# A two-layer vision tower on one core: divided softmax chain, one-pass products, moved turnings, zero products and an early weight split

## Chip, cores, metric

One core of a Trainium2 chip. The metric is the device time of one execution in microseconds, as the median of several runs.

## What is computed

Eight images of 256 x 256 are cut into 64 patches of 1024 values; a linear layer makes 192 features of each and a class token goes in front, so there are 8 x 65 = 520 tokens. Two layers follow, each with attention and an expert layer, each behind a layer norm and added to the stream `h`:

```
h = h + L0_attn(norm(h))   # squared scores plus scores, no softmax
h = h + L0_ffn(norm(h))    # 8 experts of width 768, top 2, gelu
h = h + L1_attn(norm(h))   # 12 heads of 16, all tensors quantized to 8 bits
h = h + L1_ffn(norm(h))    # 8 experts of 128 and 8 of 256, top 8, gelu
```

The second attention quantizes queries, keys, values and scores by global minimum and maximum, and its softmax is an integer one:

```
x_int = round(x / scale); x_int = x_int - max(x_int, axis=-1)
x0_int = floor(-LN2 / scale); x_int = maximum(x_int, N_EXP * x0_int)
qexp = floor(x_int / x0_int); r = x_int - x0_int * qexp
b_int = floor(b / a / scale); c_int = floor(c / a / (scale * scale))
e = (r * (r + b_int) + c_int) * exp2(-qexp) * (a * scale * scale)
return e / sum(e)
```

## The kernel before

The program is written out by hand, one instruction stream for each engine, with semaphores between them; the order of the text is the order on the engine. There is no planner. In a VectorE stream `then` issues a step and waits for its end, `settle` issues and only counts, `step` issues and gives the count, and `after` waits for such a count.

**Expert layers.** `ffn` goes through 48 tiles of 128 hidden columns in the first layer and 24 in the second. A tile has two halves of 260 tokens. TensorE makes the hidden values (`entry`), ScalarE the gelu, VectorE multiplies with the token's weight (L1301), ScalarE and VectorE split the product in a high and a low fp32r part (L998, L1306), and TensorE multiplies down (`project`, L597 and L659). Products in fp32r are one pass of TensorE, and the pair of parts replaces an fp32 product. TensorE's order is the up product of tile x + 2, then the down product of tile x. The weights come by DMA into one of two raw slots, one load for each first-layer expert, and are split the same way by `weights_hi` on ScalarE (L974, L976) and `weights_lo` on VectorE (L1282, L1285), three pieces for a load: the pieces of load n + 1 stand in the first three tiles of load n. Load 0 is split during the first attention. SyncE issues the loads, each behind the semaphore that its slot's last low part has raised; the first layer's load 3 stands behind the combine weights (`comb_to_dram`, `token_weights`).

**Softmax.** The scores lie in `sc`: 50 rows of 65 for each partition, two rows for the class token's queries and 48 for the patches' (12 for each of four pairs of images). For them there are four chunks, 14 rows and three times 12. While the scores come in nine groups, VectorE reduces maximum and minimum (L1507, L1508). TensorE turns the two statistics, VectorE reduces them and TensorE spreads the result (`statistics`). Then a chain of steps on one or three elements gives the scale, its reciprocal, the factor `alpha`, bounds, and the integer constants (L1512 to L1540). For each chunk ScalarE scales (L1122; GpSimd chunk 3), VectorE subtracts the row's top and clamps (`distance`, L1553 and L1554), ScalarE makes the quotient (L1128), GpSimd the power of two (L541; ScalarE chunk 3), VectorE the remainder (L1561), ScalarE the square (L1134), and VectorE the exponential (L1573). Its end raises `e_ready`: the first time behind the class rows' normalisation (L1597 to L1599), which are divided at once; the others are divided after the product.

**Products with the values.** TensorE turns a chunk's pair rows with fp32 transposes (`turn_rows`: L835 the class rows, L846 six blocks of 128, L849 the left-over first and last keys of an image, 6 rows for each parity), ScalarE and VectorE copy them out of PSUM, and `times_v` multiplies: L858 left-over keys with `v_last` (408 columns, fp32), L861 six blocks with `v_pairs`. `times_v_cls` (L871) has 16 fp32 products of 12 columns for the class token. An fp32 product stands as two records in the profile. `output` on VectorE divides and reduces for the next statistics (L1611 to L1619); L1634 to L1637 do so for the class token. `v_pairs` and `v_last` are made earlier, by ScalarE and GpSimd (L531, L533).

**Zero products.** `fill(n)` issues n bf16 products of a zero matrix with 260 zero columns, whose result nobody reads. They stand ahead of several transposes of normalised rows. Ahead of the second routing there are 50. The routing (`gate`, `route`) multiplies by the router in fp32 and turns the logits (L590).

## Time and profile before

| | us |
|---|---|
| median of 3 runs | 371.45 (371.27 to 372.63) |
| the profiled execution | 371.17 |
| its span, first to last instruction | 369.1 |
| TensorE products, busy | 298.1 (81%) |
| VectorE, busy | 268.8 (73%) |
| ScalarE, busy | 202.3 (55%) |
| GpSimd, busy | 20.8 (6%) |
| mean granted TensorE clock | 0.882 |

The profiled execution takes 2.1 us more than its span; that part lies before the first and after the last instruction. A busy share is a mean over stages with different limits: what a stage is bound by is read from its own stretch. Times in the rows are counted from the span's start. Each row of a timeline is start, duration, engine, line, operation and operands; in square brackets stands the idle time of the engine before it and who ended that.

### The profile page before, as it was taken

The page shows a single profiled execution, that of the slowest core. Times are in us where ns is not written, and L with a number is a line of the kernel's source. Part 1 is how long each engine was busy: PE and PEld are TensorE (multiplying, and loading weights), DVE is VectorE, ACT ScalarE, POOL GpSimd, SP SyncE. Part 2 cuts the span into 40 slices and gives each one's busy share as a digit, 9 for nine tenths or more (in the row PEclk, how much of TensorE's full clock was granted, in tenths as well). Part 3 has the DMA queues.
Part 4 walks back from the last instruction along what each step waited for, and adds up shares of the span by engine and source line. Part 5 has one row for each costly group of instructions (what it writes and reads, how often), then busy time and mean ns, then how long its engine had stood idle before and what let it go on. Part 6 is the DMA issues. An engine that isn't in the chain of part 4 may idle for free.

```text
span 369.1 us, 6068 instructions
## 1 busy us (share of the span) xinstructions
PE 298.1 (81%) x2294; PEld 267.2 (72%) x2294; DVE 268.8 (73%) x717; ACT 202.3 (55%) x486; POOL 20.8 (6%) x46
## 2 busy tenths in 40 slices
PE   5989998899999999999881260099439888999991
PEld 5968857799999999999781140067326278999991
DVE  1269275888888888898668989965468558888852
ACT  1034476677677686777273574660010667777750
POOL 4230000000000000000000015400000000000000
PEclk9999999999999999999996555578557699999997
DMA  6980401235044043000000000000500014444401
GB/s 201 302 275 3 151 0 45 92 133 178 16 166 168 13 151 99 2 1 2 2 0 0 2 2 0 0 2 0 199 0 3 0 33 125 149 154 134 114 7 43
DMA packets 10396, 27.37 MB, mean 74 GB/s; under 512 B 1368, under 2 KB 1992, under 8 KB 10368
## 3 DMA queue, kind: packets, MB, share of 16 engines
q1 hardware_dynamic: 9792, 26.03, 21.9%
q0 software_dynamic: 576, 0.96, 1.2%
q8 instruction: 18, 0.29, 0.3%
q14 instruction: 10, 0.08, 0.1%
HBM read 26.54 MB, written 0.45 MB: 73 GB/s over the span
## 4 chain that ended last, share of the span: by engine, by line
PE 65%; DVE 25%; ACT 5%; issue 2%; DMA 1%; DVEq 0%; ACTq 0%
PE bank L597 26%; PE bank L659 9%; PE bank L577 7%; PE bank L644 4%; PE bank L642 4%; PE bank L700 3%; PE bank L861 2%; PE bank L846 1%; DVE embed_area L1553 1%; ACT hid_hi L998 1%; DVE bn L1204 1%; PE bank L858 1%; DVE group_lo L1508 1%; DVE row_hi L1507 1%; DVE stat_q L1428 1%
## 5 line engine op out<-in xcount | busy, mean ns | idle before, releaser
L597 PE MATMUL bank<-hid_hi,pj_parts 128*128 128x260 f32 x288 | 76.1, 285 | 1.7 <-DVE hid_lo L1306 1.7
L998 ACT ACTIVATE hid_hi<-hidden_area 128x260 fp32r<-128x260 f32 x144 | 55.9, 422 | 38.8 <-DVE hidden_area L1301 37.5
L1306 DVE TENSOR_TENSOR hid_lo<-hidden_area,hid_hi 128x260 fp32r<-128x260 f32 x144 | 56.6, 427 | 10.0 <-ACT hid_hi L998 0.9
L597 PEld LDWEIGHTS bank<-hid_hi,pj_parts 128*128 128x128 f32 x288 | 54.1, 188 | 2.5 <-DVE hid_lo L1306 2.0
L991 ACT ACTIVATE hidden_area<-bank 128x260 f32<-128x260 f32 x144 | 49.2, 377 | 5.7 <-PE bank L644 4.7
L597 PE MATMUL bank<-xt_hi,fc_hi 128*128 128x260 f32 x144 | 41.6, 289 | 1.4 <-ACT hidden_area L989 1.3
L644 PE MATMUL bank<-xt_lo,fc_lo 128*128 128x260 f32 x144 | 41.4, 288 | 0.0
L659 PE MATMUL bank<-hid_hi,pj_parts 128*128 128x260 f32 x144 | 40.7, 283 | 0.0
L659 PE MATMUL bank<-hid_lo,pj_parts 128*128 128x260 f32 x144 | 40.7, 282 | 0.0
L597 PE MATMUL bank<-hid_lo,pj_parts 128*128 128x260 f32 x144 | 40.7, 282 | 0.0
L597 PE MATMUL bank<-xt_lo,fc_hi 128*128 128x260 f32 x144 | 40.7, 282 | 0.0
L642 PE MATMUL bank<-xt_lo,fc_hi 128*128 128x260 f32 x144 | 40.6, 282 | 0.0
L597 PE MATMUL bank<-xt_hi,fc_lo 128*128 128x260 f32 x144 | 40.4, 281 | 0.0
L1301 DVE TENSOR_TENSOR hidden_area<-hidden_area 128x260 f32<-128x260 f32 x72 | 28.0, 424 | 7.0 <-ACT hidden_area L989 6.1
L1301 DVE TENSOR_TENSOR hidden_area<-hidden_area,xn 128x260 f32<-128x260 f32 x72 | 28.1, 423 | 2.2 <-ACT hidden_area L991 1.7
L597 PEld LDWEIGHTS bank<-xt_hi,fc_hi 128*128 128x128 f32 x144 | 27.2, 189 | 1.9 <-ACT hidden_area L989 1.5
L1282 DVE TENSOR_TENSOR fc_lo<-raw_area,fc_hi 128x768 fp32r<-128x768 f32 (+1 forms) x28 | 23.5, 844 | 5.4 <-ACT fc_hi L974 4.3
L597 PEld LDWEIGHTS bank<-hid_lo,pj_parts 128*128 128x128 f32 x144 | 27.3, 190 | 0.0
L597 PEld LDWEIGHTS bank<-xt_lo,fc_hi 128*128 128x128 f32 x144 | 27.1, 189 | 0.1
L597 PEld LDWEIGHTS bank<-xt_hi,fc_lo 128*128 128x128 f32 x144 | 27.1, 188 | 0.0
L659 PEld LDWEIGHTS bank<-hid_lo,pj_parts 128*128 128x128 f32 x144 | 27.1, 188 | 0.0
L659 PEld LDWEIGHTS bank<-hid_hi,pj_parts 128*128 128x128 f32 x144 | 27.1, 188 | 0.0
(299 smaller groups left out, 571.0 us busy)
## 6 DMA issues: line engine op xcount, KB each, us to landing
raw_area<-fc_dram SPq DMA_DIRECT2D x8, 768.0 KB, 4.3
raw_area<-pj_dram SPq DMA_DIRECT2D x8, 576.0 KB, 5.4
xn<-comb_dram SPq DMA_DIRECT2D x12, 260.0 KB, 3.4
raw_area<-fc_dram SPq DMA_DIRECT2D x6, 512.0 KB, 4.1
embed_area<-embed_in_dram SPq DMA_DIRECT2D x8, 352.0 KB, 8.2
hidden_area<-comb_dram SPq DMA_DIRECT2D x9, 260.0 KB, 3.3
raw_area<-pj_dram SPq DMA_DIRECT2D x6, 384.0 KB, 4.4
score_area<-w_l_dram SPq DMA_DIRECT2D x1, 576.0 KB, 11.8
```

The source lines that it names most:

```text
L577: last = pe.matmul(out, lhs(kc), rhs(kc), start=(kc == 0), stop=(kc == KC - 1))
L597: mm = pe.matmul(out, lhs[a], rhs[b], start=start and n == 0, stop=stop and n == 2, skip_group_check=True)
L642: pe.matmul(out, fc_hi[:, s, 1, cols], x_mix[:, tok], start=False, stop=False, skip_group_check=True)
L644: mm = pe.matmul(out, fc_lo[:, s, 1, cols], x_mix[:, tok], start=False, stop=True, skip_group_check=True)
L659: mm = pe.matmul(PB[SUMS[2 + n]][:, 0:HALF], pj_tails[:, s, j], hidden[:, x % 3, tok], start=x == 0 and part == 0, stop=part == 1, skip_gr ...
L700: mm = pe.matmul(PB[i][:, 0:D], patches[:, k, i * 128:(i + 1) * 128], w_tok[:, k, :], start=(k == 0), stop=(k == TOKK - 1))
L861: last = pe.matmul(PB[4 + i][:, k * 4 * (HD + 1):(k + 1) * 4 * (HD + 1)], e_t[:, HC * i + k, :], v_pairs[:, i, 2 * k:2 * k + 2, :, :].rear ...
L991: act.activation(hid[:, x % 2, tok], src, ACT.Gelu_apprx_tanh).then_inc(entry_out[y], 1)
L998: act.activation(hid_hi[:, x % 3, tok], hid_w[:, x % 2, tok], ACT.Copy).then_inc(hid_hi_ready[y], 1)
L1282: dve.tensor_tensor(lo, raw, hi.bitcast(F32), ALU.subtract).then_inc(w_lo_done[s], 1)
L1301: dve.tensor_tensor(hid_w[:, x % 2, tok], hid[:, x % 2, tok], tok_w[tile.weights][:, tok], ALU.mult).then_inc(weighted[y], 1)
L1306: dve.tensor_tensor(hid_lo[:, x % 3, tok], hid_w[:, x % 2, tok], hid_hi[:, x % 3, tok].bitcast(F32), ALU.subtract).then_inc(hid_lo_ready[y ...
```

## The change

1. *Early split.* All six pieces of load 1 are split during the first attention: the high parts behind those of load 0 on ScalarE, the low parts on VectorE between the squared scores and the residual update. Tiles 0 to 2 of the first expert layer have no pieces left.
2. *Scalar chain.* `qk` and `qk_step` are made among the nine groups of reductions. The bound below (`sa_lo`) is gone: scores and tops are only cut from above. The integer constants run interleaved with the tops, and their last five steps (`exp_floors`) stand between the two halves of chunk 0's distance.
3. *Order of the chunks.* VectorE makes chunk 0's exponential and the class rows ahead of chunk 1's remainder and chunk 3's distance. ScalarE copies the class rows and chunk 0's turned rows between the squares and quotients.
4. *One-pass products.* Exponentials of the class rows and the left-over keys are split into a high part (ScalarE's copy) and a low part (VectorE: `e_cls_lo`, `e_last_lo`), both fp32r. The low part of the left-over keys takes 38 further partitions, at 64 and up, against the same values, so L858 is one fp32r product; `v_last` then has 102 partitions, and the turning of these values four small products instead of two. The low part of the class rows takes 12 further columns, so the 16 class products have 24 columns each, in fp32r, and the mask has 24.
5. *Order on TensorE.* In `times_v` the left-over keys come last. `times_v(0)` stands before the third turning, `times_v(1)` before the fourth.
6. *Zero products.* 36 ahead of the first turning, from the first quotient on, and 5 ahead of the second. Ahead of the second routing 46, then a wait for the variances, then 14, instead of 50.
7. *Places.* Some tensors lie elsewhere (`v1_flat` in `hid_hi`, `e_cls` and `e_last` in `hid_lo`, `logits_t` in the hidden area).

```diff
-LR = 38
+LR = 102
+TWICE = 2 * 12
...
+        v1_flat = hid_hi[0:S].rearrange("p a c -> p (a c)")[:, 0:B * D].rearrange("p (b d) -> p b d", b=B)
...
+        hid_lo_words = hid_lo[:].rearrange("p a c -> p (a c)")
+        e_cls = hid_lo_words[0:S, 0:256].rearrange("p (r q) -> p r q", r=2)
+        e_last = hid_lo_words[0:LR, 256:768].rearrange("p (i q) -> p i q", i=4)
...
+        v_last = sb("v_last", [LR, 4, NH, 2, HD + 1], F32R)
...
-        o_cls_m = sb("o_cls_m", [DC, B * KC, NH])
+        o_cls_m = sb("o_cls_m", [DC, B * KC, TWICE])
...
-                                    pe.matmul(bank[0:m, at:at + DC // 2], even, own[0], start=True, stop=True)
-                                    last = pe.matmul(bank[m:z, at:at + DC // 2], odd, own[1], start=True, stop=True)
+                                    at = ((b % 4) * KC + kc) * (DC // 2)
+                                    for row, n_rows, key, q in ((0, 32, 0, 0), (32, 32, S - 1, 1), (64, 32, 0, 0), (96, HC, S - 1, 1)):
+                                        last = pe.matmul(bank[row:row + n_rows, at:at + DC // 2],
+                                                         v[:, key:key + 1].broadcast_to([DC, n_rows]), own[q],
+                                                         start=True, stop=True)
...
-                    pe.wait_ge(e_cls_ready, 1)
+                    pe.wait_ge(e_cls_lo_ready, 1)
                 if c >= 2:
                     pe.wait_ge(et_act, ET_ACT[c - 2])
+                    pe.wait_ge(e_last_lo_ready, 2 * (c - 1))
...
+                for k in range(HC):
+                    pe.matmul(PB[4 + i][:, k * 4 * (HD + 1):(k + 1) * 4 * (HD + 1)], e_t[:, HC * i + k, :],
+                              v_pairs[:, i, 2 * k:2 * k + 2, :, :].rearrange("p h b d -> p (h b d)"),
+                              start=k == 0, stop=False, skip_group_check=True)
                 pe.wait_ge(v_last_ready, 5 * (i + 1))
+                pe.wait_ge(e_last_lo_ready, 2 * (i + 1))
                 pe.matmul(PB[4 + i][:, 0:PAIR_COLS], e_last[:, i, :], v_last[:, i].rearrange("p h b d -> p (h b d)"),
-                          start=True, stop=False, skip_group_check=True)
-                for k in range(HC):
-                    last = pe.matmul(PB[4 + i][:, k * 4 * (HD + 1):(k + 1) * 4 * (HD + 1)], e_t[:, HC * i + k, :],
-                                     v_pairs[:, i, 2 * k:2 * k + 2, :, :].rearrange("p h b d -> p (h b d)"),
-                                     start=False, stop=True, skip_group_check=True)
-                last.then_inc(pv_mm, 1)
+                          start=False, stop=True, skip_group_check=True).then_inc(pv_mm, 1)
...
-                        at = (2 * b + kc) * NH
-                        last = pe.matmul(PB[1][0:DC, at:at + NH], v1_flat[:, b, kc * DC:(kc + 1) * DC],
-                                         e_cls[:, b // 4, SLOT * (b % 4):SLOT * (b % 4) + NH], start=True, stop=True)
+                        at = (2 * b + kc) * TWICE
+                        last = pe.matmul(PB[1][0:DC, at:at + TWICE], v1_flat[:, b, kc * DC:(kc + 1) * DC],
+                                         e_cls[:, b // 4, SLOT * (b % 4):SLOT * (b % 4) + TWICE], start=True, stop=True)
...
             pe.wait_ge(v1_ready, 10)
+            pe.wait_ge(quot_ready, 1)
+            fill(36, 6)
             turn_rows(0)
+            fill(5, 6)
             turn_rows(1)
+            times_v(0)
             turn_rows(2)
-            times_v(0)
+            times_v(1)
             turn_rows(3)
-            times_v(1)
             times_v(2)
             times_v_cls()
             times_v(3)
...
-            fill(50, 1)
+            fill(46, 1)
+            pe.wait_ge(mv_ready, 4)
+            fill(14, 1)
...
-                    if j <= 2 and load + 1 < LOADS:
+                    if load and j <= 2 and load + 1 < LOADS:
...
-            for piece in range(3):
-                weights_hi(0, piece)
+            for first in range(2):
+                for piece in range(3):
+                    weights_hi(first, piece)
...
             act.wait_ge(sq_bias_ready, 1)
             square(0)
             quotient(2)
+            act.wait_ge(et_mm, 1)
+            act.activation(e_cls[:], PB[0][0:S, 0:256].rearrange("p (r q) -> p r q", q=128),
+                           ACT.Copy).then_inc(e_cls_ready, 1)
             square(1)
+            turned_rows(0, 0)
             quotient(3)
+            turned_rows(0, 1)
             a, z = CHUNKS[3]
             act.wait_ge(quot_ready, 4)
             act.activation(pow2[:, a:z, :].bitcast(I32), quot[:, a:z, :], ACT.Copy, scale=-2.0 ** 23,
                            bias=(127 + OFFSET) * 2.0 ** 23).then_inc(last_pow2_ready, 1)
             square(2)
-            act.wait_ge(et_mm, 1)
-            act.activation(e_cls[:], PB[0][0:S, 0:256].rearrange("p (r q) -> p r q", q=128),
-                           ACT.Copy).then_inc(e_cls_ready, 1)
-            turned_rows(0, 0)
-            turned_rows(0, 1)
             square(3)
             turned_rows(1, 0)
             turned_rows(1, 1)
...
-                    if j <= 2 and load + 1 < LOADS:
+                    if load and j <= 2 and load + 1 < LOADS:
...
+            for piece in range(3):
+                weights_lo(1, piece)
...
+                if g == 0:
+                    sq, sk = (c[:, columns["s2"][0] + i:columns["s2"][0] + i + 1] for i in range(2))
+                    product = step(dve.tensor_tensor(col("qk"), sq, sk, ALU.mult))
+                if g == 1:
+                    after(product)
+                    product = step(dve.tensor_scalar(col("qk"), col("qk"), float(HD) ** -0.5, None, ALU.mult))
+                if g == 2:
+                    after(product)
+                    settle(dve.tensor_scalar(col("qk_step"), col("qk"), 1.0 / QMAX, None, ALU.mult))
...
-            then(dve.tensor_copy(g_s[:], statistics(1, 2, 128)))
...
+            g_s = statistics(1, 2, 128)
+            then(dve.tensor_copy(col("sa_top"), g_s[:, 0:1]))
+            then(dve.scalar_tensor_tensor(col("sa"), g_s[:, 1:2], col("sa_top"), col("qk_step"), ALU.add, ALU.mult))
+            then(dve.tensor_scalar(col("sa"), col("sa"), SMIN, None, ALU.max))
+            then(dve.reciprocal(col("sa_inv"), col("sa")))
             dve.tensor_tensor(col("alpha"), col("qk"), col("sa_inv"), ALU.mult).then_inc(alpha_ready, 1)
+
+            exp_t, exp_r, exp_g, exp_f = (col(n) for n in ("exp_t", "exp_r", "exp_g", "exp_f"))
+            after(step(dve.tensor_scalar(exp_t, exp_k[:], col("sa_inv"), None, ALU.mult)))
             dve.wait_ge(alpha_ready, 1)
-            zero_of("sa", g_s[:, 1:2], col("alpha"))
...
+            zero = step(dve.tensor_scalar(col("sa_z"), g_s[:, 1:2], col("alpha"), MAGIC, ALU.mult, ALU.add))
+            tops = step(dve.tensor_scalar(row_hi[:], row_hi[:], col("alpha"), MAGIC, ALU.mult, ALU.add))
+            scaled_t = step(dve.tensor_scalar(exp_t[:, 2:3], exp_t[:, 2:3], col("sa_inv"), None, ALU.mult))
+            after(zero)
+            high = step(dve.tensor_scalar(col("sa_hi"), col("magic_top"), col("sa_z"), MAGIC, ALU.subtract, ALU.add))
+            after(scaled_t)
+            rounded = step(dve.tensor_scalar(exp_r, exp_t, MAGIC, MAGIC, ALU.add, ALU.subtract))
+            after(high)
+            tops = step(dve.tensor_scalar(row_hi[:], row_hi[:], col("sa_hi"), None, ALU.min))
+            after(rounded)
+            over = step(dve.tensor_tensor(exp_g, exp_r, exp_t, ALU.is_gt))
+            after(tops)
+
+            def exp_floors():
+
+                after(over)
+                then(dve.tensor_tensor(exp_f, exp_r, exp_g, ALU.subtract))
+                then(dve.tensor_scalar(col("neg_x0"), exp_f[:, 0:1], -256.0, None, ALU.max))
+                settle(dve.tensor_scalar(col("neg_x0_30"), col("neg_x0"), float(N_EXP), None, ALU.mult))
+                then(dve.reciprocal(col("neg_inv_x0"), col("neg_x0")))
+                dve.tensor_scalar(col("quot_bias"), col("neg_inv_x0"), -0.5, OFFSET - 0.5, ALU.mult,
+                                  ALU.add).then_inc(quot_bias_ready, 1)
...
-                then(dve.scalar_tensor_tensor(neg_n[:, a:z, :], s, col("sa_lo"), top, ALU.max, ALU.subtract))
-                dve.tensor_scalar(neg_n[:, a:z, :], neg_n[:, a:z, :], 0.0, col("neg_x0_30"), ALU.min,
-                                  ALU.max).then_inc(n_ready, 1)
+                below_top = step(dve.scalar_tensor_tensor(neg_n[:, a:z, :], s, col("sa_hi"), top, ALU.min, ALU.subtract))
+                if n == 0:
+                    exp_floors()
+                after(below_top)
+                dve.tensor_scalar(neg_n[:, a:z, :], neg_n[:, a:z, :], col("neg_x0_30"), None, ALU.max).then_inc(n_ready, 1)
...
+            def e_last_lo(c):
+
+                dve.wait_ge(et_act, ET_ACT[c])
+                for p in (0, 32):
+                    src = PB[TURN_BANKS[c][1]][p:p + HC, 256:384]
+                    dve.tensor_tensor(e_last[64 + p:64 + p + HC, c, :], src, e_last[p:p + HC, c, :].bitcast(F32),
+                                      ALU.subtract).then_inc(e_last_lo_ready, 1)
+
+            def e_cls_lo():
+
+                dve.wait_ge(e_cls_ready, 1)
+                again = e_cls.rearrange("p r (b m) -> p (r b) m", m=SLOT)[:, :, NH:TWICE]
+                src = PB[0][0:S, 0:256].rearrange("p (b m) -> p b m", m=SLOT)[:, :, NH:TWICE]
+                dve.tensor_tensor(again, src, again.bitcast(F32), ALU.subtract).then_inc(e_cls_lo_ready, 1)
...
-            remainder(1)
-            settle(dve.tensor_tensor(col("poly_c"), exp_f[:, 2:3], col("half_b2"), ALU.subtract))
-            distance(3)
+            dve.wait_ge(dve_done, steps[0])
+            then(dve.tensor_tensor(col("poly_c"), exp_f[:, 2:3], col("half_b2"), ALU.subtract))
             then(exponential(0))
 
             then(dve.tensor_reduce(cls_sum[:], sc[:, 0:2, :], X, ALU.add))
             then(dve.reciprocal(cls_sum[:], cls_sum[:]))
             dve.tensor_tensor(sc[:, 0:2, :], sc[:, 0:2, :], cls_sum[:].unsqueeze(2).broadcast_to([128, 2, S]),
                               ALU.mult).then_inc(e_ready, 1)
+            remainder(1)
+            distance(3)
+            e_cls_lo()
+            exponential(1).then_inc(e_ready, 1)
             remainder(2)
-            exponential(1).then_inc(e_ready, 1)
+            e_last_lo(0)
             remainder(3)
             exponential(2).then_inc(e_ready, 1)
             exponential(3).then_inc(e_ready, 1)
...
+            e_last_lo(1)
             turned_rows(2)
+            e_last_lo(2)
             output(0)
             turned_rows(3)
+            e_last_lo(3)
             output(1)
             output(2)
...
-            src = PB[1][0:DC, 0:B * KC * NH].rearrange("p (b j h) -> p b j h", b=B, j=KC)
-            own = cls_mask[:, :, 0:NH].unsqueeze(1).broadcast_to([DC, B, KC, NH])
+            src = PB[1][0:DC, 0:B * KC * TWICE].rearrange("p (b j h) -> p b j h", b=B, j=KC)
+            own = cls_mask[:, :, 0:TWICE].unsqueeze(1).broadcast_to([DC, B, KC, TWICE])
```

## Rows read from the trace of the kernel before

**Rows 1.** The page's time slices: the granted TensorE clock in tenths.

```profile
PEclk9999999999999999999996555578557699999997
```

**Rows 2.** Busy time in stretches (columns: stretch, length, engines, clock, DMA).

```profile
72.00:177.00 105.00, 104.54 (x866) 104.54 (x867) 88.14 (x206) 77.18 (x198) 0.00 (x0) 1.00 0.25 86
```

**Rows 3.** Timeline of TensorE (start, duration, line, what), first expert layer's start.

```profile
63.08 0.36 PE L597 MATMUL bank<-hid_hi,pj_parts 128*128 128x260 f32 x1 [0.31 <-DVE hid_lo L1306]
...
72.46 0.39 PE L597 MATMUL bank<-hid_hi,pj_parts 128*128 128x260 f32 x1 [0.98 <-DVE hid_lo L1306]
...
79.79 0.28 PE L597 MATMUL bank<-hid_hi,pj_parts 128*128 128x260 f32 x1
```

**Rows 4.** Timeline of VectorE, the softmax and its outputs.

```profile
223.00 0.38 DVE L1518 TENSOR_TENSOR consts<-consts 128x1 f32<-128x1 f32 x1
...
227.44 1.16 DVE L1553 SCALAR_TENSOR_TENSOR embed_area<-score_area,consts,row_hi 128x910 bf16<-128x910 f32 x1
228.64 0.46 DVE L1554 TENSOR_SCALAR embed_area<-embed_area,consts 128x910 bf16<-128x910 bf16 x1
...
230.53 0.90 DVE L1587 TENSOR_TENSOR consts<-consts 128x1 f32<-128x1 f32 x1
...
239.05 0.29 DVE L1599 TENSOR_TENSOR score_area<-score_area,cls_sum 128x130 f32<-128x130 f32 x1
...
243.84 1.03 DVE L1573 SCALAR_TENSOR_TENSOR score_area<-score_area,consts,raw_area 128x780 f32<-128x780 f32 x1 [0.73 <-ACT score_area L1134]
...
263.07 0.34 DVE L1619 TENSOR_REDUCE stat_o<-embed_area 128x1 f32<-128x192 f32 x1
```

**Rows 5.** Timeline of TensorE, products with the values.

```profile
251.14 0.95 PE L858 MATMUL bank<-attn_area,hidden_area 38*128 38x408 f32 x2
...
253.41 3.82 PE L871 MATMUL bank<-attn_area,raw_area 65*96 65x12 f32 x32
...
258.82 2.83 PE L861 MATMUL bank<-embed_area,attn_area 128*128 128x68 f32 x12
```

**Rows 6.** Timeline of TensorE, first and second routing.

```profile
50.16 1.73 PE L560 MATMUL bank<-ident,xn 128*128 128x128 f32 x10 [0.46 <-DVE xn L1230]
...
55.46 0.43 PE L590 MATMUL bank<-ident,logits_t 8*128 8x8 f32 x5
...
278.57 7.52 PE L567 MATMUL bank<-zeros 128*128 128x260 bf16 x50
287.80 2.06 PE L560 MATMUL bank<-ident,xn 128*128 128x128 f32 x10 [1.71 <-DVE xn L1230]
...
296.06 0.44 PE L590 MATMUL bank<-ident,logits_t 16*128 16x16 f32 x5
```

**Rows 7.** Timeline of ScalarE, first attention.

```profile
30.02 1.15 ACT L976 ACTIVATE pj_parts<-raw_area 128x1152 fp32r<-128x1152 f32 x1
33.07 0.49 ACT L1044 ACTIVATE attn_area<-bank 65x384 f32<-65x384 f32 x1 [1.91 <-PE bank L577]
```

**Rows 8.** Timeline of VectorE, first attention.

```profile
35.43 1.42 DVE L1285 TENSOR_TENSOR pj_parts<-raw_area,pj_parts 128x768 fp32r<-128x768 f32 x2
...
44.23 0.56 DVE L1412 SCALAR_TENSOR_TENSOR h<-bank,h 128x384 f32<-128x384 f32 x1 [4.52 <-PE bank L577]
```

**Rows 9.** Timeline of GpSimd, the softmax.

```profile
230.42 1.01 POOL L541 TENSOR_SCALAR raw_area<-hidden_area 128x910 int32<-128x910 bf16 x1 [3.94 <-ACT hidden_area L1128]
```

**Rows 10.** Busy time in stretches, as rows 2, late softmax and second routing.

```profile
251.20:253.00 1.80, 1.80 (x12) 1.22 (x11) 1.63 (x5) 0.00 (x0) 0.00 (x0) 1.00 0.00 0
254.00:255.00 1.00, 1.00 (x15) 1.00 (x14) 0.93 (x4) 0.00 (x0) 0.00 (x0) 1.00 0.00 0
255.00:256.00 1.00, 1.00 (x9) 1.00 (x8) 0.34 (x2) 0.00 (x0) 0.00 (x0) 0.50 0.00 0
257.20:258.40 1.20, 1.20 (x3) 0.46 (x2) 0.94 (x4) 0.00 (x0) 0.00 (x0) 0.50 0.00 0
...
289.00:290.00 1.00, 1.00 (x6) 0.60 (x7) 0.41 (x2) 0.55 (x4) 0.00 (x0) 0.56 0.00 0
```

51 lines of the change are left out of this document (19 added, 32 removed).

## The prediction

> **What bounds the kernel now.** I read the page's row of the granted clock first, then tables by stage, then each engine's instructions at the stages that the diff touches. In the page TensorE's clock is full in the first half, at half from about slice 22 to 29, and mixed until slice 31 [rows 1]. The long stretch in the first half is bound by TensorE alone: 104.5 of 105 us busy at full clock [rows 2], so nothing inside it can gain, but what lies at its start moves all that follows. So I look for time in three places.
>
> (1) The start of the first expert layer. Tile 0's down product starts at 63.08, tile 3's at 72.46, tile 6's at 79.79: three tiles take 9.38 us first and 7.33 us afterwards [rows 3].
>
> (2) The integer softmax, 219 to 263 us. First only VectorE, ScalarE and GpSimd work, in a chain of small dependent steps and then chunk passes. The first exponentials are handed over at 239.34, the last at 244.87, and the stage's last reduction ends at 263.41 [rows 4]. The last 18.5 us are TensorE's: two-part fp32 products, of which the last group runs at half clock [rows 5].
>
> (3) The second routing: from the first transposes to the turned logits 287.80 to 296.06, where the first routing needs 50.16 to 55.46 [rows 6].
>
> **The early load (start of the first expert layer).** Six conversions of load 1 leave tiles 0 to 2. On ScalarE they go behind load 0's: two of 0.8 us and one of 1.15 us [rows 7] are about 2.6 us. They start at 31.1 and end at 33.7; the first value copy started at 33.07 after an idle of 1.91 us [rows 7], and its successors have gaps, so this 0.6 us is absorbed before TensorE needs all four copies. On VectorE the low parts cost 0.9 + 0.9 + 1.42 = 3.2 us and stand in front of the residual update, which came at 44.23 after 4.52 us of idle [rows 8]: hidden, with 1.3 us over. If TensorE finished earlier than before, up to that much would show. No DMA is issued elsewhere in SyncE's program; load 3's slot is free earlier, but its issue stands behind the four combine-weight rows, so it just goes right behind them at about 63. Gain: the start pattern falls back to the steady one, 9.38 - 7.33 = **2.05 us** [rows 3]; from above 2.2, from below 1.2 (if half of the start delay is fill-up of the pipeline and not conversions).
>
> **The scalar chain.** Before, the scale's last step starts at 223.00 and the first chunk pass at 227.44: 13 dependent steps [rows 4]. Two steps ahead of the scale go among the reductions, where nothing waits but three issues cost about 0.2 us. Behind the scale some six steps stand in series now instead of 13; at 4.44 / 13 = 0.34 us each they take 2.1 us, and I give 0.3 for the long ones over the row maxima. So the scale comes at about 223.1, and the first chunk pass at 225.4. But five steps (floors, reciprocal, quotient bias) now stand between its two halves: 5 x 0.19, less one hidden, 0.8. The second half ends at 229.10 before [rows 4] and at about 227.6 now: **-1.5** (between -2.0 and -0.6: the steps at 0.15 or at the 0.38 of the row at 223.00).
>
> **The reordered chunks.** In front of the first hand-over, one remainder pass and chunk 3's distance go behind it: 0.95 each for their passes over 780 values (1.03 less the overlap, as in the row at 243.84), and 0.8 for the distance's second half, which alone is 0.46 in the row at 228.64 but lay against GpSimd. That is -2.7 more. Against it stands the port. A step on one element took 0.90 us at 230.53 [rows 4] while GpSimd's power pass ran from 230.42 to 231.43 [rows 9]. GpSimd now starts its first two passes against the same VectorE steps, only earlier, so I keep that loss. The first hand-over comes at 239.34 - 1.5 - 2.7 = 235.1. By a rule of the Trainium skill (page "SBUF — State Buffer", section on who interferes with whom) an operation with two SBUF inputs and a GpSimd operation that reads SBUF shut each other out for whole instructions; a sum without it would be 1.0 us better, and the row at 230.53 agrees with it.
>
> For the last hand-over the same work is in front of it as before, plus three small subtractions (class 0.25, left-over keys 0.35, all from PSUM; from 0.15 to 0.5 each), less the idle of 0.73 in front of the last pass [rows 4]: 244.87 - 1.5 - 0.7 + 0.6 = **243.2**. ScalarE now waits for TensorE in the middle of its chunk work (class copy ahead of a square, turned rows ahead of a quotient), and VectorE's left-over subtraction waits for ScalarE ahead of a remainder. That is a ring through TensorE's zero products; what is queued behind them is the whole softmax.
>
> **The zero products.** 260 columns take 0.217 us at 1.2 GHz and 0.109 at 2.4. They start when the first quotient lands, at about 228.8. The 50 ahead of the second routing began at half clock and took 7.52 us, between the 10.9 and 5.4 of the two levels, because the clock rose among them: 0.15 each [rows 6]. 36 then take 5.4 us and, as the slow ones come first, some 0.7 more: 234.9, at the latest, all at half, 236.6. The first hand-over is at 235.1: nothing or up to 1.5 us late. I take 0.
>
> **The products.** From 253.41 on, 32 half products of the class token take 3.82 us, and the last twelve 2.83, all or mostly at half clock (0.50 in 255 to 256) [rows 5, 10]. A left-over product takes 0.95 in two records at full clock [rows 5]; as one fp32r record of 408 columns it is a quarter, 0.24, bounded by 0.12 (three tiles of 20 fp32r products of 260 columns take 7.33) [rows 3] and 0.95. "FP8 and Floating Point Precision" (the Trainium skill, its list on native precision) says that true fp32 takes four passes, which gives the same 0.24; no row shows an fp32r product of this shape. Sixteen class products of 24 columns: 0.067 each (15 records in the microsecond at full clock) to 0.12 (3.82 / 32), so 1.1 to 1.9; I take 1.3, by the nearest row [rows 10].
>
> With this TensorE leaves the end of the path. Products 0 follow the second turning, and from the last hand-over VectorE's own list is longer: two left-over subtractions and a copy of turned rows 0.35 + 0.65 + 0.35, output 0 at 1.72 (1.63 busy in a window of 1.8) [rows 10], copy and subtraction 1.0, outputs 1 and 2 at 3.45, the class block 1.25 (0.94 for half of the columns) [rows 10], output 3 at 1.75, and 0.5 for three waits: 11.0. 243.2 + 11.0 = 254.2 against 263.41: **-9.2 us**. TensorE in parallel: at full clock the last product ends near 251, 1.2 us ahead of its reader. That margin is the cover of the fp32r guesses and of a late zero product; without it each costs its size.
>
> **The second routing.** Instead of 50 products 46, then a wait for the variances and 14 more (1.5 us at full clock) that end at about 287.4, ahead of the normalised rows at 287.8. Before, they ended at 286.1, the queue stood still 1.7 us, and the clock fell in 289 to 290 (0.56) [rows 6, 10]. If it holds, the stretch costs what the first routing costs: 8.26 - 5.30 = **-2.9 us** [rows 6] (bounds: -3.0, and +0.8 if the clock rises so late that the 14 end after the rows are ready). The wider router matters little, as moving columns are the same. If the clock is up, the four small transposes and output products between 265 and 278 might gain 0.3; I take nothing.
>
> **The sum.** -2.05 - 9.2 - 2.9 = -14.15. The profiled execution took 371.17 (span 369.1): 357.0. The median of the runs is 0.28 above it: **357.3 us**.
>
> **The rivals.**
> *The clock falls again between the turnings* (15 of 100). TensorE is idle about 1.6 us before the second turning and again before the third; the fall in 289 to 290 came after an idle of this length, and another at 255 under the 12-column products [rows 10]. At half clock for 5 us the products end 2.5 later, of which 1.2 is covered, and thin class products would add 1: 359.5.
> *The second routing stays at half clock* (10 of 100). From 289 on the gate's fp32 products and the zero products behind them ran at half clock and did not raise it in time [rows 6]. Then -2.9 is gone: 360.2.
> *The ring* (8 of 100): the zero products end after the first hand-over and ScalarE's squares wait for a turning: +1.5 at the first, +1 through the left-over subtraction: 359.8.
> *Slower* (2 of 100): zeros do not lift the clock at the new places. Then 36 take 7.8 us, every turning and product runs at half; the stage ends near 263.0 (-0.4), and 60 x 0.217 = 13.0 us in front of the second routing, from 278.6, end at 291.6, 3.8 late. With -2.05 this is +1.35: 372.8. It decides from a rise later than some 7 us behind the first zero product. Against it: the 50 took 7.52 us and not 10.9 [rows 6].
> *The change does not do what it says* (3 of 100), the early load or the order leaves the path as it is: 362.
>
> **How the numbers follow.** The forecast has 62 of 100, its own range 355.2 to 359.2. From 357.3 the bounds of the parts reach down to 354.3 and the likelier rivals up to 361.3; that is the range. A difference under 0.5% (1.9 us) is no change for a measurement of this kernel. Only the slower rival and combinations near it are not faster: faster 0.96, same 0.02, slower 0.02.
>
> **What would show it.** Tile 3's down product 7.3 us after tile 0's. First hand-over at 233.1 in the new trace's time (2.05 earlier), last at about 241.2, last output reduction near 252.2 with VectorE busy before it, TensorE at full clock from the end of the zero products on. Turned logits 5.4 us behind the first transposes. Wrong it would be with a half clock in any stretch behind the zero products, a VectorE idle of more than 1 us between the last hand-over and output 3, or class products above 2 us.

## The result, and the profile after

The changed kernel took **358.53 us** (median of 4 runs, 357.54 to 362.10) against 371.36 (4 runs, 370.55 to 372.63): ratio 0.967 with an interval of 0.960 to 0.974. The ratios, here and below, leave disturbed executions out, the medians don't. The forecast was 357.3, from 354.3 to 361.3. The profiled execution took 357.54 with a span of 355.7, against 371.17 and 369.1: -13.6 us, where the sum said -14.15. (The spans differ by 13.4: 2.2 ahead of the softmax, 8.3 in it, 2.9 behind it.) Measured again beside the experiments, the same kernel gave a median of 362.03 (6 runs, 357.23 to 364.08, ratio 0.969, interval 0.962 to 0.976), above the range. So the median moved by 3.5 us between two measurements of one kernel, which is more than it is off in the first (1.2); this has a section of its own below.

The page's rows of the clock and of TensorE, after. They answer to [rows 1]: the mixed middle is gone, and two half-clock blocks with a full one between them are left.

```profile
PEclk9999999999999999999999555599557999999996
PE   5989998999999999999986053579139979999991
```

The first expert layer, TensorE, as [rows 3]: tile 0's down product and, three tiles on, tile 3's, now 7.31 us apart instead of 9.38.

```profile
63.15 0.36 PE L601 MATMUL bank<-hid_hi,pj_parts 128*128 128x260 f32 x1 [0.30 <-DVE hid_lo L1321]
...
70.46 0.28 PE L601 MATMUL bank<-hid_hi,pj_parts 128*128 128x260 f32 x1
```

VectorE in the softmax and behind it, as [rows 4]. The last reduction of the scores' maxima comes first; all distances below are from its end, 216.95 (219.16 before).

```profile
216.41 0.54 DVE L1534 TENSOR_REDUCE row_hi<-score_area 128x6 f32<-128x390 f32 x1
...
220.10 0.18 DVE L1553 TENSOR_TENSOR consts<-consts 128x1 f32<-128x1 f32 x1
...
222.02 1.95 DVE L1591 SCALAR_TENSOR_TENSOR embed_area<-score_area,consts,row_hi 128x910 bf16<-128x910 f32 x1
...
224.60 0.58 DVE L1595 TENSOR_SCALAR embed_area<-embed_area,consts 128x910 bf16<-128x910 bf16 x1
...
232.46 0.31 DVE L1653 TENSOR_TENSOR score_area<-score_area,cls_sum 128x130 f32<-128x130 f32 x1
...
238.77 2.13 DVE L1613 SCALAR_TENSOR_TENSOR score_area<-score_area,consts,raw_area 128x780 f32<-128x780 f32 x2
241.19 0.60 DVE L1627 TENSOR_TENSOR hid_lo<-bank,hid_lo 6x128 fp32r<-6x128 f32 x2 [0.29 <-ACT hid_lo L1161]
241.82 0.69 DVE L1619 COPY attn_area<-bank 128x512 f32<-128x512 f32 x1
242.55 0.60 DVE L1627 TENSOR_TENSOR hid_lo<-bank,hid_lo 6x128 fp32r<-6x128 f32 x2
...
249.82 0.55 DVE L1694 TENSOR_TENSOR o_cls_m<-bank,cls_mask 96x384 f32<-96x384 f32 x1
...
252.53 0.34 DVE L1676 TENSOR_REDUCE stat_o<-embed_area 128x1 f32<-128x192 f32 x1
```

The first hand-over (end of the step at 232.46) is at 232.77, the last (end of the pass at 238.77) at 240.90, the last output reduction at 252.87. From the last hand-over on VectorE has one gap, the 0.29 at 241.19.

TensorE in the same stretch and in the second routing, as [rows 5, 6].

```profile
226.56 6.25 PE L571 MATMUL bank<-zeros 128*128 128x260 bf16 x36 [7.33 <-ACT hidden_area L1143]
...
245.55 1.45 PE L880 MATMUL bank<-hid_lo,hid_hi 65*96 65x24 f32 x16
246.85 1.80 PE L867 MATMUL bank<-embed_area,attn_area 128*128 128x68 f32 x12
248.40 0.69 PE L872 MATMUL bank<-v_last,hid_lo 102*128 102x408 f32 x1
...
252.92 0.38 PE L695 MATMUL bank<-ident,stat_o 128*10 128x128 f32 x1 [3.83 <-DVE stat_o L1676]
...
268.02 8.96 PE L571 MATMUL bank<-zeros 128*128 128x260 bf16 x60
277.25 1.82 PE L564 MATMUL bank<-ident,xn 128*128 128x128 f32 x10 [0.27 <-DVE xn L1245]
...
282.67 0.44 PE L594 MATMUL bank<-ident,hidden_area 16*128 16x16 f32 x5
```

TensorE's last product ends at 249.09, and the engine then waits 3.83 us for VectorE: the end of the stage has changed engines. The turned logits come 5.42 us behind the first transposes instead of 8.26. And the clock in stretches, as [rows 2]:

```profile
230.00:232.00 2.00, 2.00 (x16) 1.61 (x15) 1.90 (x5) 1.04 (x1) 0.21 (x1) 0.78 0.00 0
232.00:248.00 16.00, 13.81 (x120) 11.23 (x118) 14.96 (x32) 9.01 (x20) 0.63 (x1) 1.00 0.00 0
248.00:272.00 24.00, 9.89 (x49) 6.64 (x49) 17.77 (x54) 1.20 (x4) 0.00 (x0) 0.50 0.21 77
```

The clock falls at 248, under the last group of value products, about 1 us before TensorE is done. The prediction named a half clock in any stretch behind the zero products as a sign of being wrong, so this sign came; what it cost is taken up below.

### The profile page after: what moved, and what is told of

It reads as the page before. It is cut to its first block, busy times and chain, and to the rows that moved or that the text cites. A ratio compares the mean times of both kernels' runs of the same rounds, so it can differ in the third digit from the quotient of the medians.

```text
span 355.7 us, 6206 instructions
## 1 busy us (share of the span) xinstructions
PE 293.6 (83%) x2357; PEld 266.6 (75%) x2357; DVE 270.4 (76%) x725; ACT 202.6 (57%) x486; POOL 21.0 (6%) x46
## 4 chain that ended last, share of the span: by engine, by line
PE 62%; DVE 28%; ACT 5%; issue 2%; DMA 1%; DVEq 0%; ACTq 0%
PE bank L601 28%; PE bank L663 10%; PE bank L581 7%; PE bank L648 5%; PE bank L646 5%; PE bank L704 4%; DVE embed_area L1591 1%; DVE bn L1219 1%; DVE group_lo L1535 1%; DVE row_hi L1534 1%; DVE score_area L1601 1%; DVE stat_q L1455 1%; DVE stat_q L1456 1%; PE bank L564 1%; DMA embed_area<-embed_in_dram 1%
## 5 line engine op out<-in xcount | busy, mean ns | idle before, releaser
L601 PEld LDWEIGHTS bank<-hid_hi,pj_parts 128*128 128x128 f32 x288 | 54.1, 188 | 0.5 <-issue 0.5
L648 PE MATMUL bank<-xt_lo,fc_lo 128*128 128x260 f32 x144 | 41.5, 288 | 0.0
L571 PE MATMUL bank<-zeros 128*128 128x260 bf16 x235 | 32.1, 299 | 7.4 <-ACT hidden_area L1143 7.3
L571 PEld LDWEIGHTS bank<-zeros 128*128 128x128 bf16 x235 | 24.2, 106 | 13.8 <-issue 8.5
```

The costliest lines, as they stand in the source:

```text
L571: pe.matmul(PB[bank][:, 0:HALF], zeros[:, 0:128], zeros[:], start=True, stop=True, skip_group_check=True)
L601: mm = pe.matmul(out, lhs[a], rhs[b], start=start and n == 0, stop=stop and n == 2, skip_group_check=True)
L648: mm = pe.matmul(out, fc_lo[:, s, 1, cols], x_mix[:, tok], start=False, stop=True, skip_group_check=True)
```

## The experiments

Every kernel below is the changed one with one edit; best, hold_short and hold_full have more than one. The times spread by several us in each, so the table gives, beside the median, what each edit does inside the profiled execution, in us: T, the end of the last reduction of the scores' maxima (L1534) from the start of the span; from T to the end of the first hand-over, of the last hand-over, and of the last output reduction; and from there to the end of the span. T and the last two columns add to the span. The kernels ran in three groups, each on a chip of its own: again, u_early, u_fill1 and u_fill2; u_order, u_fp32, one and late; u_chain, best, hold_short and hold_full. Each ratio is to the kernel before, measured in the same group (medians 371.44, 370.88 and 370.97). The changed kernel stands only in the first group, so medians of the other two can't be held against it directly. In three profiles T is near 222: there the clock fell early, which is told below.

| kernel | median (range, runs) | ratio, interval | T | first | last | output | rest |
|---|---|---|---|---|---|---|---|
| before | 371.36 (370.55-372.63, 4) | 1 | 219.16 | 20.18 | 25.71 | 44.25 | 105.69 |
| changed | 358.53 (357.54-362.10, 4) | 0.967, 0.960-0.974 | 216.95 | 15.82 | 23.95 | 35.92 | 102.83 |
| changed again | 362.03 (357.23-364.08, 6) | 0.969, 0.962-0.976 | 216.29 | 15.82 | 23.95 | 35.93 | 102.88 |
| u_early | 359.99 (359.69-365.24, 6) | 0.972, 0.967-0.977 | 218.76 | 15.84 | 23.96 | 35.94 | 102.90 |
| u_chain | 364.25 (358.62-365.28, 6) | 0.969, 0.963-0.975 | 221.72 | 17.55 | 25.68 | 37.65 | 102.93 |
| u_order | 359.92 (358.28-360.31, 4) | 0.970, 0.966-0.975 | 218.49 | 18.49 | 24.11 | 36.74 | 102.87 |
| u_fp32 | 365.39 (361.89-367.01, 4) | 0.985, 0.979-0.990 | 222.07 | 15.83 | 23.68 | 39.88 | 102.95 |
| u_fill1 | 363.82 (361.50-366.90, 6) | 0.982, 0.976-0.987 | 216.89 | 15.82 | 23.95 | 41.91 | 102.90 |
| u_fill2 | 361.48 (359.11-369.77, 6) | 0.973, 0.967-0.978 | 217.19 | 15.83 | 23.95 | 35.93 | 105.98 |
| one | 356.73 (356.21-357.70, 6) | 0.963, 0.960-0.967 | 217.30 | 15.83 | 23.63 | 34.41 | 102.89 |
| late | 356.81 (356.41-362.02, 4) | 0.963, 0.958-0.967 | 216.96 | 14.78 | 23.17 | 35.15 | 102.89 |
| best | 361.77 (357.79-362.44, 6) | 0.974, 0.969-0.979 | 216.61 | 14.79 | 22.90 | 39.91 | 102.88 |
| hold_short | 355.46 (353.78-362.28, 6) | 0.957, 0.953-0.962 | 217.28 | 14.78 | 22.88 | 33.65 | 101.77 |
| hold_full | 355.95 (354.59-360.89, 6) | 0.961, 0.956-0.965 | 222.59 | 14.78 | 22.88 | 33.65 | 102.56 |

Where the code of a stretch and the clock are the same, the columns behind T repeat within 0.03 us, the last within 0.12. They tell the edits apart; the medians alone don't.

**The changed kernel once more.**

> The changed kernel itself, unaltered, once more: the base for the others, and a second profile of it. Its four executions so far took 357.5 to 362.1, the longer ones with a lower mean clock (0.900 against 0.911). Theory (the spread is TensorE's clock rising or falling at other moments in the stages behind 220 us): ratio to before 0.963 to 0.972, single executions again between 357 and 363, the longer ones with the lower mean clock. Rival (the spread is something else, DMA for instance): times spread without a relation to the mean clock.

Behind T the stage times are the same to 0.01 us up to the output reduction, and the median is another by 3.5 us. The relation to the mean clock held (357.23 us at 0.911, 364.08 at 0.889), two executions were longer than the 363 expected, and the profiled one was the fastest, so this run doesn't show where in the longer ones the clock fell.

**u_early: the early load undone.**

```diff
-                    if load and j <= 2 and load + 1 < LOADS:
+                    if j <= 2 and load + 1 < LOADS:
-            for first in range(2):
-                for piece in range(3):
-                    weights_hi(first, piece)
+            for piece in range(3):
+                weights_hi(0, piece)
```

> Undoes only the early split: the six pieces of load 1 stand in tiles 0 to 2 of the first expert layer again. Theory (the conversions delay three tiles and the long TensorE-bound stretch passes the delay on): 2.1 us slower than the changed kernel, about 360.5, tile 3's down product 9.4 us behind tile 0's and not 7.2. Rival (half of the delay is the pipeline filling up, which the early split only moves): 1 us or less.

```profile
62.56 0.36 PE L601 MATMUL bank<-hid_hi,pj_parts 128*128 128x260 f32 x1 [0.31 <-DVE hid_lo L1320]
...
71.94 0.39 PE L601 MATMUL bank<-hid_hi,pj_parts 128*128 128x260 f32 x1 [0.98 <-DVE hid_lo L1320]
```

TensorE's timeline in this kernel: 9.38 us from tile 0 to tile 3, the value of before to the hundredth, and 7.31 in the changed kernel. All behind it is unchanged (35.94). The medians don't show it (359.99 against 362.03 on the same chip), the fastest runs do (359.69 against 357.23).

**u_chain: the scalar chain and the two distance passes of before.**

```diff
-            g_s = statistics(1, 2, 128)
-            then(dve.tensor_copy(col("sa_top"), g_s[:, 0:1]))
...
+            then(dve.tensor_copy(gs_sb[:], statistics(1, 2, 128)))
+            then(dve.tensor_tensor(col("qk"), ...))
...
+            zero_of("sa", gs_sb[:, 1:2], col("alpha"))
...
-                if n == 0:
-                    exp_floors()
```

> The changed kernel with the scalar chain and the two distance passes as they were before (every scalar behind the one ahead of it, all of it ahead of chunk 0), the order of the chunks, the class and key products and the zero products as changed. Theory (the steps of the prediction add): the first hand-over comes 1.5 to 1.7 us later after the last score reduction (15.82 us in the changed kernel, 20.18 before; with the order alone undone 18.49, so 1.69 is left for the chain), the last output reduction 35.92 + 1.6 = 37.5 us, time +1.6. Rival (chunk 0 isn't what the hand-over waits for, so that the chain's gain is only waiting moved to ScalarE's quotient): first hand-over within 0.4 us of 15.82, time the same.

The first hand-over, the last and the output reduction all come 1.73 us later (17.55, 25.68, 37.65). The theory holds, and none of the chain's gain is lost on the way.

**u_order: the chunks in their old order.**

```diff
             distance(2)
+            remainder(1)
...
+            distance(3)
...
             then(exponential(0))
...
-            remainder(1)
-            distance(3)
```

(And the later remainders back in their old order, and ScalarE's copies of the class rows and of chunk 0's turned rows behind square 2, as before.)

> Undoes only the order of the chunks on VectorE and ScalarE (first exponential behind chunk 1's remainder and chunk 3's distance again, ScalarE's copies of the class rows and chunk 0 behind the third square); scalar chain, products and zero products stay. Theory (the stage's end is VectorE's own list behind the last hand-over): first hand-over 2.7 us later against the first quotient, but the last within 0.5 us, and the last output reduction 0.5 to 1.5 us later, since TensorE has more left to do then. Rival (the early turnings are what brought the gain, as TensorE is the bound): the last output reduction 3 us or more later. In the profile the distance from the scores' statistics (their transpose on TensorE) to the last output reduction is 34.9 us in the changed kernel.

The first hand-over is 2.67 us later, the last 0.16, the output reduction 0.82. The order is worth what was worked out for the first hand-over, but two thirds of it are gone at the end, since the passes are only moved behind it.

**u_fp32: class and left-over key products in fp32 as before.**

```diff
-LR = 102
-TWICE = 2 * 12
+LR = 38
+TWICE = 12
...
-            e_cls_lo()
-            e_last_lo(0)
```

> Undoes only the one-pass products: class and left-over exponentials in fp32 as before, without the low parts, 12 class columns, 38 partitions. Theory (VectorE loses 0.63 us for each of three subtractions on its list, but TensorE needs 0.6 us more for each left-over product and 1 to 2.5 more for the class products, and is the bound then): the last output reduction 1 to 3 us later than in the changed kernel. Rival (VectorE's list stays the bound even then): 1.5 to 2 us earlier, so the fp32r products would be a loss. 34.9 us from the scores' statistics to the last output reduction in the changed kernel.

The output reduction comes 3.96 us later, more than the 1 to 3 expected. VectorE's groups of this kernel, 219 to 262 us (columns: line, shapes, count, busy and mean, then idle before and its releaser) show who is waited for, and TensorE's timeline why:

```profile
L1663 DVE RECIPROCAL o_inv<-bank 128x24 f32<-128x24 f32 x4 | 1.2, 302 | 3.9 <-PE bank L869 3.9
...
L1686 DVE TENSOR_TENSOR o_cls_m<-bank,cls_mask 96x192 f32<-96x192 f32 x1 | 0.4, 354 | 2.2 <-PE bank L877 2.2
```

```profile
255.72 2.81 PE L865 MATMUL bank<-embed_area,attn_area 128*128 128x68 f32 x12
258.46 1.73 PE L869 MATMUL bank<-attn_area,hidden_area 38*128 38x408 f32 x2
```

TensorE sets the end again, and its last group falls into half clock, as in [rows 5]. So without the fp32r products 4 us of the 8.3 are gone, because TensorE is the bound again. Such amounts don't add up: the four edits of this stage (chain 1.73, order 0.82, fp32r 3.96, zero products 6.0) make 12.5 together, since each is measured with the others in place.

**u_fill1: no zero products ahead of the turnings.**

```diff
-            pe.wait_ge(quot_ready, 1)
-            fill(36, 6)
-            fill(5, 6)
```

> Undoes only the zero products of the softmax, the 36 ahead of the first turning and the 5 ahead of the second. Theory (they lift the clock, and the turnings and products need it): the turnings run at half clock and the last output reduction ends 3 to 8 us later against the first hand-over, so 361 to 366. Rival (VectorE's own list bounds this stage, and the clock rises by itself within some 6 us of the first turning): at most 1 us slower, 359.5, the last output reduction within 1 us of where it is, 20.1 us behind the first hand-over.

```profile
232.00:240.00 8.00, 6.26 (x31) 4.71 (x31) 7.73 (x14) 6.14 (x11) 0.58 (x1) 0.50 0.01 2
240.00:248.00 8.00, 8.00 (x39) 6.55 (x39) 4.91 (x12) 1.88 (x7) 0.00 (x0) 0.50 0.00 0
248.00:256.00 8.00, 8.00 (x44) 7.69 (x40) 5.27 (x17) 0.80 (x3) 0.00 (x0) 0.50 0.08 10
```

The hand-overs don't move (15.82, 23.95); the outputs come 6.0 us later. TensorE was busy 16 of 16 us in the last two stretches, with the small products of the real work, and the clock stayed at 0.50. So in this kernel the full clock from 231 to 248 comes from the zero products. It is no rule for real work: in the kernel before, which has no zero products there, the clock rose at 244.75, 5.3 us behind its first turning, under three chunks' turnings in a row:

```profile
244.00:245.00 1.00, 1.00 (x6) 0.93 (x6) 0.89 (x2) 0.98 (x4) 0.00 (x0) 0.62 0.00 0
```

The changed kernel puts products between its turnings. No run undoes this order on TensorE, so whether it is the order that keeps u_fill1's clock down, or chance, isn't shown.

**u_fill2: 50 zero products ahead of the second routing, no split.**

```diff
-            fill(46, 1)
-            pe.wait_ge(mv_ready, 4)
-            fill(14, 1)
+            fill(50, 1)
```

> Undoes only the zero products ahead of the second routing: 50 in one piece again, no wait for the variances, no 14 more. Theory (TensorE's standstill behind the 50 drops the clock during transposes and router products): 2.8 us slower than the changed kernel, about 361.2, turned logits 8.3 us behind the first transposes, granted clock 0.5 there. Rival (the clock there is a matter of luck and in the changed kernel it only happened to hold): the stretch stays at 5.4 us, and the time is that of the changed kernel within 0.5 us.

```profile
277.52 0.73 PE L564 MATMUL bank<-ident,xn 128*128 128x128 f32 x3 [1.32 <-DVE xn L1243]
...
285.32 0.63 PE L594 MATMUL bank<-ident,hidden_area 16*128 16x16 f32 x5
```

```profile
276.00:277.50 1.50, 0.20 (x2) 0.00 (x0) 1.36 (x8) 0.51 (x2) 0.00 (x0) 1.00 0.00 0
277.50:280.00 2.50, 2.37 (x14) 1.34 (x15) 1.73 (x6) 1.91 (x8) 0.00 (x0) 0.93 0.00 0
280.00:285.00 5.00, 4.98 (x14) 1.24 (x14) 2.08 (x4) 3.19 (x4) 0.00 (x0) 0.50 0.00 0
```

TensorE stands still 1.32 us, and 2 us later the clock falls, with the engine busy again: 7.80 us to the turned logits and 105.98 to the end, +3.1. The theory holds, with 7.80 for the 8.3 expected.

**one: one copy and one subtraction for both blocks of left-over keys.**

```diff
-                for p in (0, 32):
-                    src = PB[TURN_BANKS[c][1]][p:p + HC, 256:384]
...
+                src = PB[TURN_BANKS[c][1]][0:32 + HC, 256:384]
+                dve.tensor_tensor(e_last[64:LR, c, :], src, e_last[0:32 + HC, c, :].bitcast(F32), ...)
```

> Changed kernel with one copy and one subtraction for the left-over keys in place of two each: they cover partitions 0 to 37 at once; the rows between the two groups then hold other finite values that meet zeros in the values' matrix. Theory (VectorE's list behind the last hand-over is the bound, three subtractions at 0.63 stand in it): each shrinks to about 0.33, the last output reduction comes 0.9 us earlier against the last hand-over (11.1 and not 12.0 us), the kernel gains 0.9 us. Rival (ScalarE or TensorE takes over as the bound at once): 0.3 us or less.

The two groups of VectorE, 219 to 254 us, of the changed kernel and of this one:

```profile
L1627 DVE TENSOR_TENSOR hid_lo<-bank,hid_lo 6x128 fp32r<-6x128 f32 x8 | 2.3, 285 | 0.5 <-ACT hid_lo L1161 0.3
```

```profile
L1626 DVE TENSOR_TENSOR hid_lo<-bank,hid_lo 38x128 fp32r<-38x128 f32 x4 | 1.1, 284 | 0.1
```

38 partitions cost what 6 cost (284 and 285 ns). Four subtractions less (1.2 us) and 0.4 us less of idle time give -1.51 at the output reduction, where -0.9 was expected: 0.32 of it comes already ahead of the last hand-over, by chunk 0's subtraction and copy, and 1.19 behind it. It is the term of my sum that was too small, taken away.

**late: GpSimd makes the value rows of chunks 2 and 3 behind its powers of two.**

```diff
+            last_values(0)
+            last_values(1)
...
+            last_values(2)
+            last_values(3)
 
         @block.tensor
```

> Changed kernel with GpSimd's left-over values of image pairs 2 and 3 made behind its third power pass and not ahead of the softmax. Theory (chunk 0's first distance pass, 1.95 us in the changed kernel and 1.16 before, is shut out by GpSimd's operations on these values, an exclusive hold for whole operations): the pass takes 1.2 us or less, the first quotient comes 0.7 us earlier; the ten small operations then lie against later passes and give back 0.2 to 0.6 us. Rival (the pass was slow for another reason, for instance ScalarE reading the same scores): it stays above 1.8 us.

GpSimd's timeline in the changed kernel, and VectorE's first distance pass in this one:

```profile
221.73 1.27 POOL L535 TENSOR_TENSOR v_last<-attn_area,last_mask 102x96 fp32r<-102x96 f32 x4
222.98 1.08 POOL L537 TENSOR_SCALAR v_last<-last_mask 102x24 fp32r<-102x24 f32 x1
224.02 0.91 POOL L542 TENSOR_SCALAR score_area<-score_area,consts 128x780 f32<-128x780 f32 x1
```

```profile
221.90 1.17 DVE L1596 SCALAR_TENSOR_TENSOR embed_area<-score_area,consts,row_hi 128x910 bf16<-128x910 f32 x1
```

In the changed kernel VectorE's pass stands from 222.02 to 223.97. Three of GpSimd's four operations on 96 columns start after it, at 222.04, 222.35 and 222.66, and keep their usual length (the four take 1.27); the small one at 222.98, which takes 0.22 or 0.23 elsewhere, then takes 1.08 and ends with the pass. Read by starts and lengths, the pass waited for the three, and the small one for the pass; the trace shows only the lengths, not the wait itself. Out of their way the pass takes 1.17 instead of 1.95 us, and the rival is out. The first hand-over is 1.04 earlier, the output reduction 0.77: 0.27 are given back, as expected, while GpSimd's moved operations lie beside later passes and take up to 1.1 us each. The section on who interferes with whom in the Trainium skill ("SBUF — State Buffer") says that an operation with two SBUF inputs and a GpSimd operation that reads SBUF shut each other out; these rows agree.

**best: one and late together.**

> Both small improvements together: one copy and one subtraction for the left-over keys of a chunk instead of two, and GpSimd's value rows of chunks 2 and 3 moved behind its powers of two. Alone they shortened the stretch from the end of the last score reduction to the end of the last output reduction from 35.92 us to 34.41 and 35.15. Theory (VectorE's list sets this stretch to its end): the gains add, 35.92 - 1.51 - 0.77 = 33.6 us, span near 353.5 and time near 355.5, 2 us under the changed kernel. Rival (the two gains come out of one slack, or GpSimd's late value rows lie beside VectorE's work behind the last hand-over and give the gain back): 34.4 us or more, time 356.7 as the first of them alone.

Hand-overs at 14.79 and 22.90, as the sum of the two edits says (14.79 and 22.85), but the output reduction at 39.91 instead of 33.6. Neither theory nor rival foresaw that. The stretches of this kernel say why:

```profile
234.00:235.00 1.00, 0.00 (x0) 0.00 (x0) 1.00 (x3) 0.95 (x2) 1.00 (x2) 1.00 0.00 0
235.00:236.00 1.00, 0.83 (x8) 0.67 (x10) 1.00 (x2) 1.00 (x4) 1.00 (x2) 1.00 0.00 0
236.00:237.00 1.00, 1.00 (x10) 0.78 (x10) 0.94 (x3) 1.00 (x2) 1.00 (x3) 0.86 0.00 0
237.00:238.00 1.00, 1.00 (x7) 1.00 (x6) 1.00 (x2) 0.63 (x2) 1.00 (x2) 0.50 0.00 0
```

After 1.64 us of idle time ahead of the second turning the clock falls at 236.7, and is back only at 277.7. That is my first rival, "the clock falls again between the turnings", in person. The idle time alone doesn't decide it: in u_order TensorE stood still for 2.29 us between the zero products and its first turning (to 237.04), and the clock held until 250.3. The next kernel has the same code up to here, stood still for 1.23 us, keeps its clock, and reads 33.65, the additive 33.64.

**hold_short and hold_full: zero products in TensorE's idle stretches behind the last product**, on top of best (16, 16 and 18 of them, or 32, 32 and 38).

```diff
             times_v(3)
+            fill(16, 0)
             statistics(2, stat_o[:], 10, 128)
+            fill(16, 0)
...
+            fill(18, 0)
             statistics(3, stat_y[:], 4, 128)
```

> The kernel of both improvements, with 16, 16 and 18 zero products put into TensorE's three idle stretches behind the last values product (3.83, 3.95 and 4.59 us idle in the changed kernel, at granted clock 0.50). At half clock one takes 0.21 us: 16 x 0.21 = 3.4 us, so they fit in the idle time either way and cost nothing. Theory (the clock is down from 248 us because TensorE stands idle): with them it stays at 1.0, and the small products on the path (0.38 + 0.59 + 1.09 + 1.87 + 0.37 + 0.58 = 4.9 us) take about half, -2 us. Rival (the clock falls before the idle time, with the 12-column products, at 248, and so few products don't raise it again): 0.50 to 268 us as without them, time same as the kernel without them within 0.5 us.

> As the one before with 32, 32 and 38 zero products: at full clock 0.11 us each, 3.5 us, which fills the idle stretches to their ends. Theory (the clock follows TensorE's idleness): it stays at 1.0 from 232 us through the second routing, -2 us against the kernel without them. Rival (the clock has fallen before the first of these stretches, and comes back only late): the products run at half clock, 32 x 0.21 = 6.7 us against 3.8 of idle time, and the statistics behind them are late by (6.7 - 3.8) + (6.7 - 3.95) + (8.0 - 4.6) = 9 us at most, some 3 to 5 us if the clock rises within the first or second stretch.

Three stretches of hold_short, then two of hold_full (its T is 5.3 us later):

```profile
250.00:252.00 2.00, 0.57 (x3) 0.38 (x3) 1.18 (x4) 0.00 (x0) 0.00 (x0) 0.99 0.91 269
252.00:254.00 2.00, 2.00 (x11) 1.38 (x11) 1.63 (x11) 0.00 (x0) 0.00 (x0) 0.50 0.78 309
...
256.00:258.00 2.00, 0.89 (x11) 0.75 (x12) 0.28 (x2) 1.20 (x4) 0.00 (x0) 1.00 0.00 0
```

```profile
270.00:274.00 4.00, 3.94 (x35) 3.51 (x36) 3.25 (x12) 0.00 (x0) 0.00 (x0) 1.00 0.03 6
...
278.00:280.00 2.00, 2.00 (x11) 1.34 (x9) 1.82 (x10) 0.93 (x3) 0.00 (x0) 0.50 0.00 0
```

Neither story of mine held whole. With few zero products the clock goes down and up between 0.5 and 1.0; with many it stays at 1.0 from the turnings to 277.8. There the 46 zero products, at full clock from their start, are done at 275.64, TensorE stands still for 1.97 us until the variances are there, and the clock falls under the 14. The transposes of the second routing start at 280.44, 0.9 us after their first rows are ready. The rest of the span shrinks from 102.88 to 101.77 and 102.56, not by 2: of the small products at full clock only 0.9 and 0.7 us show up to the next statistics. Still hold_short has the lowest median, 355.46 us, and 353.78 at its fastest; its ratio of 0.957 (0.953 to 0.962) just meets the interval of the changed kernel and overlaps hold_full's. In the profile it differs from best mainly by the clock not falling at the turnings, which its own zero products come too late to cause; what they earn is the 1.1 us. Whether the same fall makes the distance of the medians isn't shown.

## Why the prediction was right, step by step

The total is off by 0.5 us in the profiled execution. The terms come out near theirs, with two misses that cancel inside the scalar chain, one count that was wrong, and one sign of being wrong that came and was covered.

**The early load, -2.05.** Right: 9.38 - 7.31 = 2.07, and u_early gives 9.38 back.

**The scalar chain, -1.5.** 1.73 by u_chain, inside the bounds, by two misses that cancelled. The first pass starts 5.07 us behind T instead of 8.28 (-3.2, where I had -2.0). The scale's last step comes 3.15 behind T instead of 3.84, where I had it 0.1 later and not 0.7 earlier: the two steps moved among the reductions do shorten the path. From there to the first pass it is 1.92 instead of 4.44, where I had 2.3. But the pass took 1.95 us instead of 1.16, held by GpSimd's value rows. That these two came out at -1.5 is luck. I had charged the port for the step that stood in it before, and missed that the chain, made shorter, runs into GpSimd's earlier work.

**The order, -2.7 at the first hand-over.** 2.67 by u_order. The first hand-over came 4.36 us earlier behind T (-4.2), the last 1.76 (-1.7).

**VectorE's list behind the last hand-over, 11.0 us.** The step that was off: it is 11.97. I took one subtraction of 0.35 per chunk of left-over keys; there are two, for the two blocks of rows, 0.60 together, three times (+0.75); the rest are small excesses of the outputs and the class block, less 0.2, since of the 0.5 for waits only 0.29 was needed. With it the gain of this stage is 44.25 - 35.92 = 8.3 us and not 9.2. The kernel "one" takes this out again.

**The products.** 1.45 us for the 16 of the class (1.3), 0.43 in the record of the left-over one (0.24), though the product behind it starts after 0.27. TensorE's last product ended at 249.09; the forecast in the new trace's time was 248.95. That it leaves the end of the path is shown by its idle 3.83 us and by u_fp32. But the forecast had full clock to the end, and the clock fell at 248. The last twelve products took 1.80 us (1.55 at full clock) and the left-over one 0.69 (0.43), some 0.5 us more. It cost nothing at the output reduction, because output 3 started only at 251.15. The mechanism was wrong in this last microsecond, and the margin that the prediction named covered it.

**The zero products.** They took 6.25 us, where the sum had 6.1, and ended at 232.81 against a hand-over at 232.77. u_fill1 shows what they carry in the changed order: 6.0 us.

**The second routing, -2.9.** -2.84 in the profile, 3.1 by u_fill2.

**The rivals.** "The second routing stays half", "the ring" and "it doesn't do what it says" are out in both profiles of the changed kernel. "Slower" needed the zero products not to lift the clock; they did in all twelve profiles that have them, before the 36 had ended. "The clock falls again between the turnings" (15 of 100) didn't come in the changed kernel's two profiles but is real: it is what best's profiled execution shows. Its price was wrong: I let the clock come back after 5 us (+2.2), and there it stayed down for 41 us, +6.3.

## The spread of the runs

The changed kernel took 357.23 us at a mean clock of 0.911 and 364.08 at 0.889. Two falls of the clock seen in the traces are of the size of this difference. One is best's, above. The other lies far ahead of the edit, in three profiles of fourteen; u_chain's stretches, where the changed kernel has 1.00 in all of them:

```profile
38.00:42.00 4.00, 3.92 (x47) 3.81 (x45) 3.48 (x6) 2.05 (x7) 0.00 (x0) 0.94 0.80 322
42.00:46.00 4.00, 4.00 (x16) 3.94 (x15) 1.15 (x3) 1.03 (x4) 0.00 (x0) 0.50 0.00 0
46.00:50.00 4.00, 4.00 (x16) 2.56 (x15) 2.38 (x8) 0.00 (x0) 0.00 (x0) 0.50 0.00 0
50.00:54.00 4.00, 4.00 (x21) 3.16 (x21) 1.97 (x14) 2.11 (x9) 0.00 (x0) 0.50 0.00 0
```

The clock falls at 41.5 us though TensorE is busy 3.9 of every 4, and T comes near 222 instead of 217, +5. The transfers of 322 GB/s ahead of it aren't the reason by themselves: the changed kernel moved 331 GB/s there and kept its clock. What decides is open. Which event hit which run that wasn't profiled can't be told, so I can't say that the median of 362.03 has no part in the edited stage; the changed code is equally fast there in both its profiles.

## What to carry to other kernels

Add up the list of the engine that comes next: here it decided the gain (8.3 us) more than what was taken from TensorE, and its error was a count, two instructions where I read one. Where an engine's chain becomes shorter, look at what the others do in the stretch that it moves into. Name the signs of being wrong ahead of time, and look for each one even where the time comes out right: the half clock at 248 was such a sign, and only a margin hid it. Compare stage times inside the traces when the runs spread; there 0.16 us can be told apart that no median here would show.
